# Keys, values and the first queries of an attention made inside the scan loop of a decoder layer, and kept in DRAM

## What is computed

```python
# Mamba: h is the state, 16 numbers for each of 512 channels
dA = jnp.exp(d_t[..., None] * A)
h = dA * h + (d_t * u_t)[..., None] * b_t[:, None, :]
y = jnp.einsum('bdn,bn->bd', h, c_t)
...
# feed-forward (1024 hidden, Gelu), then cross-attention with 16 heads of 16:
# q from the normalised tokens, k and v from the context; softmax over 1601 rows
# then the experts: slots = softmax over tokens, outputs mixed by softmax over slots
```

## Time and profile before

| | us |
|---|---|
| median of 3 runs (1643.01 to 1645.91) | 1644.81 |
| the profiled execution | 1639.34 |
| its span, first to last instruction | 1637.5 |
| PE busy | 1359.1 |
| ACT busy | 913.6 |
| DVE busy | 770.3 |
| POOL busy | 406.7 |

### The profile page before, as it was taken

One profiled execution on the slowest core, in us unless ns is written; L12 is line 12 of the kernel. 1 busy time (PEld: TensorE's weight loads), 2 busy tenths in 40 slices (PEclk: granted clock), 3 DMA queues, 4 the chain that ended last, 5 costly groups with the idle time before them and its releaser, 6 DMA issues.

```text
span 1637.5 us, 15369 instructions
## 1 busy us (share of the span) xinstructions
PE 1359.1 (83%) x5571; PEld 642.8 (39%) x5571; DVE 770.3 (47%) x845; ACT 913.6 (56%) x1268; POOL 406.7 (25%) x290
## 2 busy tenths in 40 slices
PE   6477578787888859897725999999999988979999
PEld 2122134353434424554521223223223234558887
DVE  3899989979997998205610001001001016561011
ACT  4536445655574436012425997998998954760310
POOL 0556655554565564104130000000000001000000
PEclk9779888899899979879756999999999988989999
DMA  5323332332233232201994000000000000010801
GB/s 190 112 80 138 121 108 95 130 103 90 90 130 103 103 128 90 53 0 39 107 108 48 1 1 1 1 1 0 0 0 0 0 0 1 1 52 17 343 13 39
DMA packets 35631, 107.95 MB, mean 66 GB/s; under 512 B 3650, under 2 KB 14146, under 8 KB 32915
## 3 DMA queue, kind: packets, MB, share of 16 engines
q1 hardware_dynamic: 35572, 107.19, 23.3%
HBM read 93.60 MB, written 2.36 MB: 59 GB/s over the span
## 4 chain that ended last, share of the span: by engine, by line
PE 49%; DVE 21%; ACT 16%; issue 8%; DMA 5%; SPq 2%; POOL 0%; DVEq 0%; ACTq 0%; POOLq 0%
DVE ps L904 11%; PE ps L1591 10%; PE ps L1576 9%; ACT arena L739 6%; PE ps L1395 4%; PE ps L1700 4%; PE ps L1350 3%; DMA arena<-arena 3%; PE ps L1741 3%; DVE arena L915 3%; ACT ps L595 2%; PE ps L1729 2%; PE ps L1281 2%; PE ps L1718 2%; PE ps L1295 1%
## 5 line engine op out<-in xcount | busy, mean ns | idle before, releaser
L739 ACT ACTIVATE arena<-ps,bound 128x1024 f32<-128x1024 f32 (+1 forms) x416 | 420.8, 1213 | 26.3 <-PE ps L1576 26.2
L439 POOL TENSOR_TENSOR arena<-arena 128x1024 f32<-128x1024 f32 x128 | 300.6, 2349 | 250.3 <-DVE arena L915 212.9
L904 DVE TENSOR_TENSOR_SCAN ps<-ps,arena 128x1024 f32<-128x1024 f32 x128 | 300.7, 2349 | 25.8 <-ACT ps L595 15.7
L1350 PE MATMUL ps<-arena,ident 128*128 128x512 f32 x512 | 255.7, 641 | 56.8 <-DVE arena L915 56.7
L1576 PE MATMUL ps<-arena 97*128 (+3 forms) x832 | 218.7, 385 | 21.9 <-issue 19.8
L1591 PE MATMUL ps<-arena 128*32 128x512 f32 (+1 forms) x1664 | 222.5, 607 | 1.1 <-ACT arena L739 0.9
L595 ACT ACTIVATE ps<-arena 128x512 f32<-128x512 f32 x256 | 166.2, 682 | 66.8 <-DVE arena L915 62.9
L426 POOL TENSOR_TENSOR rstd<-ve,mhalf 128x4 f32<-128x4 f32 (+3 forms) x18 | 23.4, 1302 | 632.5 <-DVE ve L1199 468.2
L1350 PEld LDWEIGHTS ps<-arena,ident 128*128 128x128 f32 x512 | 100.1, 203 | 200.0 <-issue 110.4
L1174 DVE COPY arena<-ps 128x512 f32<-128x512 f32 x16 | 11.1, 692 | 354.1 <-PE ps L1591 354.1
L915 DVE TENSOR_TENSOR arena<-ps,arena 128x1024 f32<-128x1024 f32 x128 | 156.0, 1219 | 6.8 <-DVE ps L904 0.5
(11 more groups left out here) (182 smaller groups left out, 1468.3 us busy)
## 6 DMA issues: line engine op xcount, KB each, us to landing
arena<-bc_scratch SPq DMA_DIRECT2D x128, 512.0 KB, 4.0
arena<-in_mw SPq DMA_DIRECT2D x16, 1024.0 KB, 9.6
arena<-arena SPq DMA_DIRECT2D x48, 128.0 KB, 14.8
arena<-arena SPq DMA_DIRECT2D x12, 400.2 KB, 16.7
arena<-in_w SPq DMA_DIRECT2D x2, 1024.0 KB
out<-xt SPq DMA_DIRECT2D x4, 512.0 KB, 2.9
xt<-in_x SPq DMA_DIRECT2D x1, 1536.0 KB
arena<-in_ctx SPq DMA_DIRECT2D x1, 1200.8 KB, 7.6
```

What stands on the lines that cost most here:

```text
L439: pool.tensor_tensor(dbu[:, w % DR], du[:, DP * p:DP * p + DP], over(bg[:, w // BG % 2, n % BG], DP), ALU.mult).then_inc(S["dbu_ready"], 1)
L739: act.activation(flat(prob[0:n, v % 2, 2 * h:2 * h + 2]), ps[0:n, 2 * (r % 3):2 * (r % 3) + 2, :].rearrange("p a b -> p (a b)"), ACT.Exp, ...
L904: dve.tensor_tensor_scan(decay_banks(w), decay_banks(w), flat(dbu[:, w % DR]), carry[:, DP * p, n:n + 1], ALU.mult, ALU.add).then_inc(S["s ...
L1350: last = mm(bank(x), ident[:, :], state(2 * j + s)[:, x], start=False, stop=(j % HP == HP - 1 and (j in SUMMED or s == 1)))
```

## The change

K, V and their lengths are made in chunk 0 of the scan loop, in four column pieces j: PE makes keys(j), ACT adds the bias, makes the first bf16 part kp0 and the square (key_parts), POOL takes the part from the rest (key_rest), ACT makes the next part (key_part), and SP stores each part to DRAM (kx_d). V goes by way of three staging buffers to vx_d. The queries of chunks 0 and 1 are made in chunk 3 in the same way (bias, part and square on ACT, the rest on POOL) and stored to qx_d. SP loads vx at q = 14 of chunk 3, kx and two chunks of qx after the last add_states. ctx, wk and wv are loaded at the start; wout, w1 and w2 after K and V are out, in chunk 1, as they share their place. Queries 2 and 3 are made around the last hidden layer: their projection, bias, square and length before the bound, their bf16 parts by DVE behind it. In chunk 3 the hidden layer of chunk 2 runs two steps earlier and three of its output tiles inside the loop. POOL adds every fourth pair in chunks 1 and 2 (SUMMED). Constant rows of kx and qx come from DRAM, not from long memsets. The arena is laid out anew and is 304 words longer.

```diff
-SUMMED = []
-VB = [0, 1, 2, 3, 4, 5, 0]
-VE = 3
+SUMMED = [j for j in range(NP, 3 * NP) if j % 4 == 2]
+KSENT = DK * len(TERMS)
+VPAIRS = [(b, min(2, KB - b)) for b in range(0, KB, 2)]
...
@@ sync @@
+            for dst, src in ((ctxt[0:CP], ctx_d), (wk[0:CP], wk_d), (wv[0:CP], wv_d)):
+                sp.dma_start(dst, src).then_inc(S["w_attn"], 16)
...
+            def store_keys(j, n):
+                o, w = KCOLS[j]
+                sp.wait_ge(S["k_act"], k_count(j, "kp%d" % n))
+                for r, (_, b) in enumerate(TERMS):
+                    if b == n:
+                        for k in range(DK):
+                            sp.dma_start(kx_d[HD * r:HD * r + HD, HALF * k:HALF * k + HALF, o:o + w],
+                                         kp[n][:, k, 0:w]).then_inc(S["kx_out"], 16)
...
+            def load_queries(c):
+                sp.wait_ge(S["qx_out"], 16 * KSENT * (c + 1))
+                landed = S["qx_in"] if c else S["kx_in"]
+                sp.dma_start(qx[0:XR, c], qx_d[c, 0:XR, :, :]).then_inc(landed, 16)
...
+            def load_ffn():
+                sp.wait_ge(S["vx_out"], 16 * len(VPAIRS))
+                sp.wait_ge(S["kx_out"], 16 * KSENT * len(KCOLS))
+                sp.wait_ge(S["row_out"], 16 * (NC + 1))
+                sp.dma_start(wout, wout_d).then_inc(S["w_out"], 16)
+                for dst, src in ((w1, w1_d), (w2, w2_d)):
+                    sp.dma_start(dst, src).then_inc(S["w_ffn"], 16)
+
+            def keys_and_values_out(q):
+                if q in (4, 9, 12):
+                    store_keys((4, 9, 12).index(q), 0)
+                if q in (5, 9, 13):
+                    store_keys((5, 9, 13).index(q), 1)
+                if q in (6, 10, 14):
+                    store_keys((6, 10, 14).index(q), 2)
+                if q in (14, 15, 16):
+                    store_values(2 * q - 28)
+                    store_values(2 * q - 27)
+                if q == 17:
+                    store_values(6)
+                if q in (17, 18, 19):
+                    store_keys(3, q - 17)
+                if q == 19:
+                    load_ffn()
+
+            def queries_out(q):
+                if q in (6, 11):
+                    sp.wait_ge(S["q_act"], q_count(q // 11, "qp0"))
+                    store_queries(q // 11, 0)
...
+                if q == 14:
+                    sp.wait_ge(S["delta_ready"], NC * DP)
+                    sp.wait_ge(S["vx_out"], 16 * len(VPAIRS))
+                    sp.dma_start(vx.rearrange("p b h d -> p b (h d)"), vx_d).then_inc(S["kx_in"], 16)
...
                     if i == 10 and c + 1 < NC:
                         store_bc(c + 1)
+                    keys_and_values_out(c * NS + i)
+                    if c == NC - 1:
+                        queries_out(i)
             load_c(NC * NS - 1)
...
+            sp.wait_ge(S["y_acc"], NC * NP)
+            sp.dma_start(kx[0:XR], kx_d[0:XR, :, :]).then_inc(S["kx_in"], 16)
+            sp.dma_start(kx[XR:XR + 1], kx_d[XR:XR + 1, :, :]).then_inc(S["kx_in"], 16)
+            load_queries(0)
+            load_queries(1)
...
@@ gpsimd @@
+                    if c == 0 and i in (3, 13, 21):
+                        key_rest((3, 13, 21).index(i), 0)
+                    if c == 0 and i in (6, 16, 23):
+                        key_rest((6, 16, 23).index(i), 1)
+                    if c == 1 and i in (0, 2):
+                        key_rest(3, i // 2)
+                    if c == NC - 1:
+                        if i in (2, 10):
+                            query_root(i // 10)
+                        if i in (9, 18):
+                            query_rest(i // 18, 0)
+                        if i in (11, 20):
+                            query_rest(i // 20, 1)
                     if w % 2 == 0 and w // 2 - 2 in SUMMED:
                         add_pair(w // 2 - 2)
...
-            pool.memset(vx, 0.0).then_inc(S["vx_init"], 1)
...
-            pool.memset(kx[XR:XR + 1, :, :], 1.0).then_inc(S["vx_init"], 1)
...
@@ scalar @@
+                for k in range(DK):
+                    act.wait_ge(S["k_ps"], DK * j + k + 1)
...
+                    act.activation(kf[:, k, 0:w], work(k)[:, 0:w], ACT.Identity, bias=ch("bk")[:, k:k + 1]).then_inc(S["k_act"], 1)
+                act.wait_ge(S["k_act"], k_count(j, "kf"))
+                act.activation(kp[0][:, :, 0:w], kf[:, :, 0:w], ACT.Copy).then_inc(S["k_act"], 1)
+                act.activation(ksq[:, :, 0:w], kf[:, :, 0:w], ACT.Square).then_inc(S["k_act"], 1)
...
-                    if i in (24, 26, 28, 30) and c:
+                    if i in (24, 26, 28, 30) and c and more:
                         hidden(c - 1, i - 24)
+                    if i in (22, 24, 26, 28) and not more:
+                        hidden(c - 1, i - 22)
+                    if c == 0:
+                        if i in (2, 12, 20, 31):
+                            key_parts((2, 12, 20, 31).index(i))
+                        if i in (5, 15, 22):
+                            key_part((5, 15, 22).index(i), 1)
+                        if i in (8, 17, 24):
+                            key_part((8, 17, 24).index(i), 2)
+                        if i in (11, 19, 24):
+                            key_lengths((11, 19, 24).index(i))
+                        if i >= 25:
+                            values(i - 25)
...
@@ vector @@
+                if c == NC - 1:
+                    if i in (0, 8):
+                        query_stats(i // 8)
+                    if i in (1, 9):
+                        query_variance(i // 9)
+                    if i in (4, 12):
+                        normed_query(i // 12)
...
+            gated(NC - 1, 1)
             second_residual(NC - 2)
-            gated(NC - 1, 1)
...
@@ tensor @@
+                    if not more:
+                        queries(i)
+                        if i in (21, 23, 25, 27):
+                            hidden(c - 1, i - 21)
+                            hidden(c - 1, i - 20)
+                        if i >= 29:
+                            ffn_out(c - 1, i - 29, 0)
+                            ffn_out(c - 1, i - 29, 1)
-            ffn_out(NC - 2, 2, 0)
-            ffn_out(NC - 2, 2, 1)
...
-            values(0, VE)
             turn_h1(NC - 1)
             for f in range(FB):
                 hidden(NC - 1, f)
+            turn_query(2)
```

709 lines of the change are left out of this document (433 added, 276 removed).

## The result

| | before | changed |
|---|---|---|
| median, us | 1643.9 (1643.0 to 1645.9, 4 runs) | 1552.6 (1551.9 to 1554.5, 4 runs) |
| profiled execution | 1639.3 | 1552.3 |
| its span | 1637.5 | 1550.5 |

The changed kernel takes 0.9445 of the time, 95% interval 0.9429 to 0.9461. The prediction was 1529 with a range of 1508 to 1560. The time is in the range and 24 us above the central value; between profiled executions the sum said 1524.2 and the chip 1552.3, so 28 us have to be found. Now and then the chip runs an execution in a slower state (one of the four of the run with the V stores later, 1662 us), and such executions are left out of every time given here.

The account below looks back on a forecast made before the run. Bound: VectorE in the loop, a chain of waits behind it, PE in attention. 1639.3 - 130.2 + 9.1 - 3.4 + 6.5 + 2 + 0.9 = 1524.2, raised 5.5 to 1529.7, predicted 1529 us; range 1508 to 1560.

Parts of the forecast that it names:

- my own case: Whole kernel: the prediction without its rivals, range 1512 to 1546 us, chance 0.65.
- Steps (1) to (13): Stage behind the loop: from the last multiplication to the first release of attention's bound, 95.0 us.
- step (14): End of the stage behind the loop: PE's start and first scores take 2.3 us, ending at 97.3.
- rival (b): Loop: a bulk load, vx at 107 GB/s, goes ahead of the broadcasts and holds load_c(14); +21, 1550 us, chance 0.07.
- (f): Before attention: waits taken out come back, as kx and qx land after the bound; 1610 us, chance 0.02.
- (c): Behind the loop: PE's clock stays low in hidden layer and tiles; +21, 1550 us, chance 0.07.
- Rival (e): Loop: its own transfers become serial with the scan, so slower than before; 1705 us if all exposed, chance 0.02.
- Chunk 0: First loop chunk: scans wait for POOL's products behind key_rest subtractions that wait for ACT; +9.1 us, bounds 0 and 28.
- rival (a): Loop: in-order stalls of ACT, POOL, PE and SP twice or more those found; +25 to +45 us, chance 0.13.
- The shared port: Loop: 18 more POOL operations hold DVE up in three or four more hits of up to 1.3; +2 us.
- Rival (d): Loop: every third of 18 new POOL operations stops DVE for its whole 2.35 us; +14, 1543 us, chance 0.04.
- Pair sums: Chunks 1 and 2: POOL's eight sums save PE 1.7 us at each of two places; -3.4 us, bounds -7 and +3.

Follow-up runs that it names:

- the last experiment: The kernel before, with PE's first V tiles waiting only for the context and the weights of K and V: median 1638.6 us, ratio 0.9970.

## Why the prediction was right or wrong

**The number is in the range, the account of the loop is not right.** The range reached to 1560 to take in rivals; my own case ended at 1546, and its last sentence says that a loop over 640 us would make the prediction wrong. From the first scan to the last multiplication the loop takes 643.0 us where it took 603.2, so by that sign it is wrong for the loop, which ends 41 us later and not 15. That the time falls inside is owed to the width meant for rivals of which only a part occurred, and to the stage behind the loop, which came out as walked.

**The stage behind the loop: right,** by its steps. PE's timeline of the changed kernel, out_project, hidden layer, first output tile, last projection, first scores:

```profile
709.92 7.17 PE L1680 MATMUL ps<-arena 128*128 128x256 f32 x32 [0.79 <-DVE arena L1150]
...
725.68 17.05 PE L1707 MATMUL ps<-arena 128*128 128x512 f32 x32 [0.69 <-ACT arena L747]
743.51 3.72 PE L1716 MATMUL ps<-arena 128*128 128x256 f32 x16
...
772.64 5.46 PE L1559 MATMUL ps<-arena 128*128 128x512 f32 x8
...
790.01 2.74 PE L1847 MATMUL ps<-arena 97*128 97x512 bf16 x6 [5.18 <-issue]
```

| step, end from the last multiplication | predicted | measured |
|---|---|---|
| (3) out_project | 23.8 | 23.3 |
| (6) hidden layer, Gelu, start of the tiles | 51.6 | 49.7 |
| (8) mamba_out | 74.7 | 72.8 |
| (11) project_query(3) | 86.9 | 84.3 |
| (13) first release of the bound | 95.0 | 91.4 |
| (14) first table load of attention | 97.3 | 97.35 |

Steps (1) to (13) were 3.6 us too dear, some tenths at each, and step (14) 3.6 too cheap: PE's branch and first scores took 6.0 and not 2.3, of which 5.18 are idle time that the profile puts down to issue. In the kernel before PE was idle there for 19.8 us, waiting for the queries' transfers too, so that this part could not be seen. The exact total is therefore luck; an error of 4 us is what the walk deserves.

**Loads: right.** kx and the queries were there before the bound, the load of vx made no scan wait, so rival (b) and (f) didn't happen. The output tiles ran at the upper level (3.72 us for 16) and the hidden layer but for its first 3 to 6 us (granted 0.50 from 725.6 to 729, 1.00 from 732 on): it took 17.05 us, where in the run with fewer waits for V it took 14.00 at the upper level throughout. The 16.58 us that the prediction took from the earlier trace rows held as much of the lower level already, so nothing of (c) came on top. Rival (e) would have needed waits for transfers of 115 us; there were 7.1. (Rival (f)'s price was added up wrongly: 1529 and 85 are 1614, not 1610.)

**Chunk 0: +9.1 predicted, +22.2 measured.** The walk through POOL's stalls was right. With the third piece of K in time, scans 4, 7, 17, 22 and 24 waited 1.0, 3.5, 0, 2.1 and 3.0 us, 9.7 in all (predicted 1.4, 3.2, 1.0, 1.4, 2.1 and so 9.1). What failed is the sentence on PE: "PE gets some 30 us ... where it is busy 98.7 of 151". That is a share, not a walk. In PE's order keys(2) stands behind skip, and skip behind DVE: 7.1 us here and 5.7 in chunk 1. This is the mechanism of rival (a), in-order waits that chain, though at one place and not at fourteen. The other 6 us of chunk 0 are longer DVE instructions, the next paragraph.

**The shared port: +2 predicted, 13.5 us of longer DVE instructions measured** (6.0 in chunk 0, 3.4 and 3.7 in chunks 1 and 2, 0.5 in chunk 3). I scaled the hits seen in the earlier trace rows with the number of POOL operations: three or four more of up to 1.3 us. There were some ten, of 0.7 to 2.2 us. POOL, once it has been late, works without gaps, and then a DVE instruction of the kinds above meets a product and can lose up to the rest of it. Rival (d) gave 14 us for this, so the size it named occurred, by its mechanism; of busy time, that is, since no run takes this cost away alone.

**SP: "each covered" was wrong by 5.7 us,** through the late third piece of K; with that in time it was right, as the waits were gone in that run.

**Pair sums: -3.4 predicted, about +5 measured** (chunk 1 +2.7, chunk 2 +5.9, chunk 3 -3.9, from the runs with and without). The gain at the two places where PE is the bound was there. The other six were put down as slack, but PE waited up to 6.57 us for a sum queued behind a root and a product, and its granted clock was 0.50 after that gap.

**Chunk 3: +6.5 predicted, +7.1 measured** without the sums. **The start: 0.9 against 1.3;** in the other runs of the changed kernel's variants it is between 0.4 and 1.9, so this is no test.

**Attention, counted as unchanged: +2.0.** PE's timeline in the first rounds, the changed kernel and the kernel before, the second group of eight products with V:

```profile
798.28 1.94 PE L1862 MATMUL ps<-arena 128*32 128x512 f32 x8
```

```profile
887.14 1.06 PE L1591 MATMUL ps<-arena 128*32 128x512 f32 x8
```

The lower level lasts one group longer, and about 1 us is lost there; the other 1 us I have not placed. It isn't a cost of the change: in the runs with the keys ahead of skip and with the V stores later, whose attention is the same, this group takes 1.06 and 1.07 us and the whole stretch 757.0 and 756.8, against 757.4 before the change and 759.4 here.

**The sum again,** with what the runs showed: 1637.5 - 130.2 + 22.2 + 5.7 + 4.7 + 7.1 + 1.3 + 2.0 = 1550.3, the span being 1550.5. In chunk 0, 22.2 = 7.1 (keys behind skip) + 6.4 (POOL occupied) + 4.5 (POOL and ACT waiting for each other) + 4.2 (the rest of the new work). Last, the 5.5 us by which I raised the sum because the median of before lay above its profiled execution were no constant: the changed kernel's median and profiled execution agree within 0.4. The executions of the kernel before spread over 1639.6 to 1646.2 in one session, with granted clocks of 0.903 to 0.897; such an offset can't be carried over to another kernel. That it comes from a stage at the edge between two clock levels is likely by the last experiment and not shown.

## What to carry to other kernels

When work is put into a loop that is full on one engine, walk the queue of *every* engine through the steps at which it is inserted, and ask of each new instruction what stands ahead of it and what that waits for; a busy share of 65% says nothing on it. Here one group of matmuls some lines too late cost 12.8 us of the loop, and one copy one step too late in three places 11.6. A helper engine can make the main engine's instructions longer, here by 13.5 us, even where no wait is shown: compare the busy time of the main engine, not only its idle time. And an addition moved to another engine pays only where the engine it relieves is the bound; two of eight sums paid, six cost. Last, compare the stages and not only the medians: the V stores' edit was 4.3 us faster by the median and 0.9 in the stages that it touches.
